# A decoder layer on one core: one list of steps for each engine, and the check of the feed-forward weights on ScalarE

## The reference, cut to what matters

```
z  = layernorm(x)
xs = z shifted by one token
k, v, r = (z*tm + xs*(1-tm)) @ W.T            # three 512x512 products; r through a sigmoid
wkv = recurrence over the tokens (k, v, decay, first), per channel
x1 = x + (r * layernorm(wkv)) @ Wo.T
y  = second recurrence over the tokens with k = layernorm(x1), v = ctx, per channel
xf = x1 + y
out = xf + down( silu(gate(z4)) * up(z4) ),   z4 = layernorm(xf)
```

## Time and profile before

| | |
|---|---|
| median of 3 runs | 647.29 us (646.05 to 648.07) |
| profiled execution | 647.78 us, span 645.7 us |
| TensorE busy | 549.5 us (85% of the span), 2658 products |
| VectorE busy | 524.5 us (81%), 935 instructions |
| ScalarE busy | 312.7 us (48%), 508 instructions, of them 57 table loads, 73.1 us |
| GpSimd busy | 23.9 us (4%) |
| granted TensorE clock, mean | 0.937 of full speed |
| chain that ended last | TensorE 40%, VectorE 35%, issue 15%, ScalarE 7% |

### The profile page before, as it was taken

The page is one execution under the profiler, slowest core; times in us unless marked ns, Lnnn a source line. Parts: engine busy times, 40 slices in busy tenths (PEclk is TensorE's granted clock), DMA queues, the critical chain, the costliest instruction groups (busy, mean ns, idle before and its releaser), DMA issues.

```text
span 645.7 us, 8051 instructions
## 1 busy us (share of the span) xinstructions
PE 549.5 (85%) x2658; PEld 388.7 (60%) x2658; DVE 524.5 (81%) x935; ACT 312.7 (48%) x508; POOL 23.9 (4%) x39
## 2 busy tenths in 40 slices
PE   3997572279999997789999998789999998799995
PEld 2442331166455776777454767677454767689995
DVE  5999998958998579977999579978999679994433
ACT  4426203237555337736564327745664417753231
POOL 1000000001000000001000000001000000000000
PEclk9999696569999998899999998899999998899999
DMA  8999100010020000020001000011001000000000
GB/s 315 383 358 366 60 1 0 0 34 33 0 62 4 2 32 1 1 67 33 0 17 48 1 16 16 1 65 34 1 3 62 1 3 30 0 33 2 17 17 35
DMA packets 11886, 34.72 MB, mean 54 GB/s; under 512 B 912, under 2 KB 912, under 8 KB 11664
## 3 DMA queue, kind: packets, MB, share of 16 engines
q1 hardware_dynamic: 11856, 34.37, 14.9%
HBM read 30.18 MB, written 12.85 MB: 67 GB/s over the span
## 4 chain that ended last, share of the span: by engine, by line
PE 40%; DVE 35%; issue 15%; ACT 7%; DVEq 1%; DMA 1%; POOL 0%; ACTq 0%; SPq 0%; POOLq 0%
PE gu L467 14%; PE dacc L390 9%; PE bank L376 6%; PE bank L443 6%; PE bank L365 4%; DVE t_slot L668 4%; DVE t_otile L848 2%; DVE t_st L789 2%; DVE t_slot L732 2%; DVE t_stats L641 2%; DVE t_pmax L711 2%; DVE t_slot L740 2%; DVE t_slot L796 2%; DVE t_st L735 2%; DVE t_gap L714 1%
## 5 line engine op out<-in xcount | busy, mean ns | idle before, releaser
L467 PE MATMUL gu<-t_z4h,t_gate 128*128 128x256 f32 x352 | 99.4, 312 | 21.5 <-DVE t_h L830 19.4
L467 PE MATMUL gu<-t_z4l,t_gate 128*128 128x256 f32 x352 | 92.4, 293 | 0.0
L467 PE MATMUL gu<-t_z4h,t_up 128*128 128x256 f32 x352 | 90.3, 288 | 0.0
L467 PE MATMUL gu<-t_z4l,t_up 128*128 128x256 f32 x352 | 90.0, 287 | 0.0
L467 PEld LDWEIGHTS gu<-t_z4h,t_gate 128*128 128x128 f32 x352 | 71.0, 202 | 29.7 <-DVE t_h L830 23.1
L597 ACT ACTIVATE t_silu<-gu,t_fsc 128x256 f32<-128x256 f32 x88 | 41.2, 477 | 91.3 <-PE gu L467 91.0
L390 PE MATMUL dacc<-t_down,t_hh 128*128 128x512 f32 x176 | 73.6, 418 | 5.7 <-DVE t_hl L684 5.7
L489 ACT ACT_TABLE_LOAD x57 | 73.1, 1283 | 1.7 <-PEq L912 0.7
L467 PEld LDWEIGHTS gu<-t_z4l,t_gate 128*128 128x128 f32 x352 | 71.0, 202 | 3.4 <-issue 2.2
L390 PE MATMUL dacc<-t_down,t_hl 128*128 128x512 f32 x176 | 71.7, 407 | 0.0
L830 DVE SCALAR_TENSOR_TENSOR t_h<-gu,t_fsc,t_silu 128x256 f32<-128x256 f32 x88 | 41.8, 477 | 36.4 <-ACT t_silu L597 36.0
(11 more groups left out here) (102 smaller groups left out, 897.3 us busy)
## 6 DMA issues: line engine op xcount, KB each, us to landing
t_xres<-in_x SPq DMA_DIRECT2D x8, 512.0 KB, 3.6
t_mixv<-in_ctx_t SPq DMA_DIRECT2D x4, 1024.0 KB, 5.3
out<-t_otile SPq DMA_DIRECT2D x16, 256.0 KB, 2.1
gate_words<-in_gate_t SPq DMA_DIRECT2D x1, 2816.0 KB, 17.7
up_words<-in_up_t SPq DMA_DIRECT2D x1, 2816.0 KB, 24.0
t_gate<-gate_words SPq DMA_DIRECT2D x1, 2816.0 KB, 16.2
down_words<-in_down_t SPq DMA_DIRECT2D x1, 2816.0 KB, 23.3
t_up<-up_words SPq DMA_DIRECT2D x1, 2816.0 KB, 23.8
```

Of the source, the lines that this page charges most:

```text
L467: last = pe.matmul(gu[u % 2][:, side, :], as_read(w[:, k, i * P:(i + 1) * P], exact), as_read(part[:, k, hf * HALF:(hf + 1) * HALF], exact ...
```

## The change

Each engine gets three lists of its own, for the first pass, the loop and the last stretch, and runs through these; the steps that it had no part in are not in them. The check is done on ScalarE: six copies (`weigh0` to `weigh5`), each of one half of a weight tile's low half words (2816 per partition, every second 16-bit word), converted, written as bytes into the output tile, and summed on the way into one column of `low_sums`; VectorE's `weigh` is one maximum over the six columns. `flag` now stands before `y` for TensorE and before `stat4_0` for VectorE. The instructions of all other steps are unchanged. The lists for GpSimd and SP give these two the order that they had; those of the last stretch are left out below, except for one line of TensorE's.

```diff
-F32R_LOST = (1 << 12) - 1
+U16 = mybir.dt.uint16
+U8 = mybir.dt.uint8
...
-    BODY = """
-        prod0 up0 silu0 xf_2 prod1 xf_3 silu1 up1 up2 rest0 up3 rest1 high0 high1 prod2 down0 silu2
-        silu3 stat4_1 turn4_1 high2 up4 stat1_0 z4_1 stat1 down1 prod3 turn1 high3 silu4 silu5 up5
-        rest2 mix_k mix_v rest3 down2 kv0 prod4 kv1 kv2 front0 back0 mix_r up6 high4 part0 high5
-        prod5 down3 up7 front1 back1 silu6 part1 fin0 front2 fin1 kv3 back2 silu7 prod6 part2 front3
-        back3 r0 part3 r1 rest4 r2 up8 r3 fin2 fin3 down4 tanh0 turn2 silu8 down5 down6 tanh1 tanh2
-        tanh3 rest5 prod7 prod8 high6 up9 high7 up10 rest6 stat2 high8 return2 rest7 rest8 rw silu9
-        prod9 down7 down8 wo up11 down9 x1_0 high9 down10 silu10 high10 prod10 up12 silu11 rest9
-        rest10 x1_1 x1_2 x1_3 stat3 turn3 prod11 silu12 out0 high11 xfront0 up13 prod12 silu13 up14
-        up15 rest11 silu14 xback0 prod13 down11 xpart0 high12 prod14 down12 xfront1 xfin0 rest12
-        rest13 high13 xfront2 xback1 down13 up16 up17 up18 down14 silu15 high14 xpart1 prod15 xback2
-        silu16 silu17 up19 rest14 xfin1 prod16 xpart2 xfront3 high15 prod17 xfin2 high16 rest15
-        silu18 silu19 xback3 prod18 xpart3 down15 rest16 up20 down16 high17 high18 high19 silu20
-        silu21 prod19 xfin3 y rest17 high20 rest18 up21 xf_0 xf_1 rest19 prod20 down17 down18
-        stat4_0 down19 prod21 rest20 high21 rest21 turn4_0 down20 z4_0 down21 out1
-        """.split()
-    FIRST_ORDER = """
-        stat1_0 stat1 turn1 mix_k mix_v kv0 kv1 kv2 mix_r front0 back0 part0 kv3 front1 fin0 back1
-        part1 r0 r1 front2 fin1 back2 part2 r2 front3 tanh0 r3 fin2 back3 part3 weigh0 tanh1 tanh2
-        fin3 weigh3 turn2 tanh3 stat2 weigh6 weigh9 weigh12 return2 rw weigh15 weigh18 weigh21
-        weigh24 weigh27 weigh30 wo x1_0 x1_1 x1_2 x1_3 stat3 turn3 xfront0 xfront1 xback0 xpart0
-        xback1 xfin0 xfront2 xpart1 xback2 xfin1 xfront3 xpart2 xback3 xpart3 xfin2 xfin3 y xf_0
-        xf_1 stat4_0 turn4_0 weigh flag z4_0
-        """.split()
...
+    PE_FIRST = """
+        turn1 kv0 kv1 kv2 kv3 r0 r1 r2 r3 turn2 return2 wo turn3 flag y turn4_0
+        """.split()
+    PE_BODY = """
+        up0 up1 up2 turn4_1 up3 up4 turn1 up5 up6 kv0 down0 down1 down2 kv1 kv2 kv3 r0 r1 r2 r3 up7
+        turn2 down3 up8 up9 return2 down4 wo down5 down6 turn3 up10 up11 down7 down8 up12 up13 up14 up15
+        down9 down10 up16 down11 up17 down12 down13 up18 up19 down14 down15 down16 up20 y up21 down17
+        down18 down19 turn4_0 down20 down21
+        """.split()
+    ACT_FIRST = """
+        stat1 turn1 mix_r front0 front1 part0 part1 front2 tanh0 front3 tanh1 tanh2 part2 part3 tanh3
+        weigh0 stat2 rw weigh1 weigh2 weigh3 weigh4 weigh5 stat3 xfront0 xfront1 xpart0 xpart1 xfront2
+        xfront3 xpart2 xpart3 stat4_0 z4_0 flag
+        """.split()
+    ACT_BODY = """
+        silu0 silu1 stat4_1 silu2 z4_1 high0 high1 high2 silu3 stat1 silu4 turn1 silu5 mix_r front0
+        silu6 high3 front1 high4 part0 part1 front2 front3 part2 tanh0 tanh1 tanh2 part3 tanh3 silu7
+        silu8 stat2 silu9 high5 high6 rw high7 high8 high9 stat3 xfront0 xfront1 silu10 silu11 high10
+        xpart0 silu12 silu13 high11 xpart1 silu14 silu15 high12 high13 xfront2 silu16 silu17 high14
+        high15 xfront3 xpart2 high16 silu18 silu19 high17 xpart3 high18 high19 silu20 silu21 high20
+        stat4_0 high21 z4_0
+        """.split()
+    DVE_FIRST = """
+        stat1_0 stat1 mix_k mix_v mix_r front0 front1 back0 part0 back1 fin0 part1 front2 fin1 back2
+        front3 part2 back3 part3 fin2 fin3 stat2 rw x1_0 x1_1 x1_2 x1_3 stat3 xfront0 xfront1 xback0
+        xpart0 xback1 xpart1 xfin0 xfront2 xfin1 xback2 xfront3 weigh xpart2 xback3 xpart3 xfin2 xfin3
+        xf_0 xf_1 flag stat4_0 z4_0
+        """.split()
+    DVE_BODY = """
+        xf_2 xf_3 prod0 stat4_1 stat1_0 prod1 prod2 z4_1 stat1 rest0 prod3 rest1 prod4 rest2 mix_k mix_v
+        front0 mix_r back0 front1 part0 back1 fin0 part1 front2 fin1 back2 front3 part2 prod5 back3
+        rest3 part3 rest4 fin2 fin3 prod6 prod7 stat2 rw x1_0 x1_1 x1_2 rest5 prod8 rest6 rest7 prod9
+        x1_3 stat3 rest8 rest9 xfront0 xfront1 xback0 prod10 prod11 xpart0 rest10 xback1 prod12 prod13
+        xpart1 xfin0 xfront2 xfin1 rest11 rest12 prod14 prod15 out0 xback2 rest13 rest14 xfront3 prod16
+        prod17 xpart2 xback3 rest15 rest16 xpart3 prod18 prod19 xfin2 xfin3 rest17 rest18 xf_0 xf_1
+        rest19 prod20 stat4_0 prod21 rest20 rest21 z4_0 out1
+        """.split()
...
+        low_sums = sb("low_sums", 6)
+        spill = otile[:, :, :].rearrange("p a b -> p (a b)").bitcast(U8)
...
-        def run_first(step):
-
-            for s in FIRST_ORDER:
+        def run_first(step, orders):
+
+            for s in orders[0]:
                 step(s, 0, None)
 
-        def run_rest(eng, step):
+        def run_rest(eng, step, orders):
 
             with eng.Fori(1, B) as b:
-                for s in BODY:
+                for s in orders[1]:
...
+                elif s.startswith("weigh") and s[5:]:
+
+                    n = int(s[5:])
+                    name, tile = (("gate", gate), ("up", up), ("down", down))[n // 2]
+                    if n % 2 == 0:
+                        act.wait_ge(w_in[name], 16)
+                    if n:
+                        act.wait_ge(bits_done, n)
+                    words = tile[:, :, :].rearrange("p a b -> p (a b)")
+                    some = words.shape[1] // 2
+                    low = words[:, n % 2 * some:(n % 2 + 1) * some].bitcast(U16)[:, 0::2]
+                    act.activation(spill[:, 0:some], low, ACT.Copy, accum_out=low_sums[:, n:n + 1]).then_inc(bits_done, 1)
...
-                elif s.startswith("weigh") and s[5:]:
-
-                    for n in range(int(s[5:]), int(s[5:]) + WEIGHED):
-                        name, tile = (("gate", gate), ("up", up), ("down", down))[n // NI]
-                        if n % NI == 0:
-                            dve.wait_ge(w_in[name], 16)
-                        k = n % NI * D
-                        words = tile[:, :, :].bitcast(I32).rearrange("p a b -> p (a b)")[:, k:k + D]
-                        if n < 2:
-                            dve.tensor_scalar(low_bits[:, n % 2, :], words, F32R_LOST, None,
-                                              ALU.bitwise_and).then_inc(bits_done, 1)
-                        else:
-                            dve.wait_ge(bits_done, n - 1)
-                            dve.tensor_tensor(low_bits[:, n % 2, :], low_bits[:, n % 2, :], words,
-                                              ALU.bitwise_or).then_inc(bits_done, 1)
                 elif s == "weigh":
-                    n = 3 * NI
-                    dve.wait_ge(bits_done, n)
-                    dve.tensor_tensor(low_bits[:, 0, :], low_bits[:, 0, :], low_bits[:, 1, :],
-                                      ALU.bitwise_or).then_inc(bits_done, 1)
-                    dve.wait_ge(bits_done, n + 1)
-                    dve.tensor_scalar(low_bits[:, 0, :], low_bits[:, 0, :], F32R_LOST, None,
-                                      ALU.bitwise_and).then_inc(bits_done, 1)
-                    dve.wait_ge(bits_done, n + 2)
-                    dve.reduce_max(inexact[:, :], low_bits[:, 0, :], AXIS_X).then_inc(inexact_done, 1)
+                    dve.wait_ge(bits_done, 6)
+                    dve.reduce_max(inexact[:, :], low_sums[:, :], AXIS_X).then_inc(inexact_done, 1)
                 elif s == "flag":
 
...
+    PE_LAST = """
+        up0 up1 up2 up3 up4 up5 down0 down1 down2 down3 up6 up7 up8 turn4_1 up9 up10 down4 down5 down6
...
```

More of the change, by code:

```diff
@@ L82, in decoder_layer @@
-    LATE = ["xf_2", "xf_3", "stat4_1", "turn4_1", "z4_1"]
-    FFN_STEPS = {f"{s}{u}" for s in ("up", "silu", "prod", "rest", "high", "down") for u in range(NU)}
-    F_STEPS = [s for s in BODY if s in FFN_STEPS or s in LATE or s in ("out0", "out1")]
-    EARLY = [s for s in BODY if s not in F_STEPS]
-    WEIGHED = 3
-    assert FFN_STEPS < set(F_STEPS) and len(BODY) == len(set(BODY)) and set(EARLY) < set(FIRST_ORDER)
+    FFN_KINDS = ("up", "silu", "prod", "rest", "high", "down", "out")
+    LATE = ["xf_2", "xf_3", "stat4_1", "turn4_1", "z4_1"]
@@ new lines, in decoder_layer @@
+    DVE_LAST = """
+        prod0 prod1 prod2 rest0 prod3 rest1 rest2 xf_2 xf_3 rest3 prod4 prod5 prod6 rest4 rest5 stat4_1
+        prod7 prod8 rest6 rest7 prod9 z4_1 prod10 rest8 rest9 prod11 prod12 rest10 prod13 rest11 prod14
+        rest12 rest13 prod15 out0 rest14 rest15 prod16 rest16 prod17 rest17 prod18 prod19 prod20 rest18
+        rest19 rest20 prod21 rest21 out1
+        """.split()
+    POOL_FIRST = """
+        stat1_0 stat1 stat2 stat3 stat4_0
+        """.split()
+    POOL_BODY = """
+        stat4_1 stat1_0 stat1 stat2 stat3 stat4_0
+        """.split()
@@ L90, in decoder_layer @@
+    POOL_LAST = """
+        stat4_1
+        """.split()
+    SP_FIRST = """
+        back3
```

(29 more changed lines are left out.)

15 lines of the change are left out of this document (11 added, 4 removed).

## The result

The kernel after takes 616.1 us (median of 4 runs, 615.34 to 617.67), the kernel before beside it 647.56 (4 runs): ratio 0.952, 95% interval 0.949 to 0.955. The forecast of 625.0 had the sign and seven tenths of the gain (22.3 us of 31.5); the measured time lies at the low edge of the range of 616 to 635, inside it by 0.1 us. The profiled execution is the quickest of the four: 615.34 us, span 613.5.

What follows compares the result with a forecast made beforehand. VectorE was taken to bound the first pass; in the turns VectorE and TensorE wait for each other. From 647.8 us, -6.1 - 8.5 - 6.0 - 5.5 = -26.1, with 3.3 given back -22.8, gives 625.0; range 616 to 635.

Steps and rivals of the forecast that it cites:

- First pass: Pass ahead of the loop: 2.8 us won before turn2, 1.9 before rw, 1.5 before x1_3; -6.1 us taken.
- ScalarE's copy: Weight check in the first pass: each of six summing copies takes 2.7 us, hidden up to 3.3 us a pass.
- Rival (c): First pass: ScalarE's check is slow, 4.9 us a copy, x1's normalisation waits 8 us, 633 us in all; chance 0.07.
- Rival (d): ScalarE, first pass and turns: a table load costs twice its row, 1.28 us more, 635 us in all; chance 0.01.
- First turn: Loop's first turn: -8.5 us, as xf_2 and xf_3 fall into VectorE's wait for the first silu.
- Turns two and three: Loop's later turns: -6.0 us and -5.5 us, the third less because its opening was 0.9 quicker before.
- VectorE's jump back takes 2.87 us: Loop's opening: the jump keeps this cost, and TensorE stands 5.1 us before up2 instead of 1.84.
- My walk: Stepping the new engine lists against each other with trace durations; out1 came at 423.3 instead of 429.3 us.
- rival (b): Loop's opening isn't regained: low clock delays turn1 by 1.5 to 3 us in two turns, 628 to 631; chance 0.10.
- The second recurrence: Loop stretch from xfront0 at 378.8 to out1 at 423.3 us; VectorE has 43.3 us to do, TensorE 40.4.
- Rival (a): Second recurrence keeps its old waits: a turn gains only 3 us, the first 5.5, 630.2 in all; chance 0.22.
- Allowance of 3.3 us: Loop turns: 1.1 us a turn given back from the summed gain for waits the list-by-list estimate misses.

Runs made afterwards that it cites:

- e7: The kernel after with 35 tiny VectorE memsets added behind the loop, in the last stretch; 617.9 us, ratio 0.954 to the kernel before.
- e4: The kernel after with prod0 put ahead of xf_2 and xf_3 in VectorE's loop list, as before; 620.0 us, ratio 0.958 to the kernel before.
- e5: The kernel after with 35 tiny VectorE memsets added behind rw of the first pass, ahead of the loop; 623.7 us, ratio 0.965 to the kernel before.
- e9: The kernel after with prod0 first on VectorE, rest0 before stat1 and down0 before turn1 in the loop; 623.6 us, ratio 0.964.

## Why the prediction was right, and where it was short

- **The sign and the mechanism:** right. Raw sum -26.1, measured -32.2.
- **First pass, -6.1 worked out, -8.7 measured.** x1_3 started 7.9 us earlier, not 6.2. Statistics of turn2 stand at 62.63 (63.0 said), rw at 71.30, behind ScalarE's share of rw. wo took 13.97 us for 15.38: in the execution of before its first 2.9 us, from 77.08 on, ran at a granted clock of 0.51, the lower of the two levels, and the rest at 1.00. That need not be the change's: e7 has the first pass of the kernel after, instruction for instruction, and there the first 2.9 us of wo ran at 0.50, wo takes 15.68 and the pass 129.8 instead of 127.1. Up to 2.7 us of this stage is scatter between executions, as much as the miss.
- **ScalarE's copy, 2.7 said:** 2.54 + 0.19, right; 16-bit words with a stride cost what other copies cost an element. Rival (c) is out.
- **The table load costs its row:** 59.34 to 60.63, 1.29, with 65 loads for 57. Rival (d) is out. The Trainium skill's drain of 1.38 us (ScalarE: Activation LUTs, "What ACT_TABLE_LOAD costs") shows in these rows as little as in the earlier trace rows.
- **First turn, -8.5 said, -8.54 measured;** e4 shows that 3.7 of it are xf_2 and xf_3 in the wait for the first silu.
- **Turns two and three, -6.0 and -5.5 said, -7.6 and -7.0 measured.** The step that failed is "VectorE's jump back takes 2.87 us", carried over from the earlier trace rows as if it belonged to the loop. It depends on what stands ahead of it, and the change had taken 37 instructions from there. With the dear jump, in e5, the step holds in detail (a wait of 5.16, 5.1 said), but the turns are 142.9 and 142.8: -4.4 and -3.5, not -6.0 and -5.5. My walk was too hopeful by 1.6 and 2.0, and lost the 1.6 ahead of the second recurrence, which begins 98.3 us behind the loop's entry (364.39 - 266.05) where 96.8 was said: turn1 comes 18.6 us after the loop's entry (284.61 - 266.05) instead of 17.5 as before, and so out1 143.0 us (409.08 - 266.05) where 141.3 was said. All of up2 runs at the low clock there, 0.41 us a product where the others take 0.28, and the 1.0 us lost at turn1 is not won back: a part of rival (b).
- **The second recurrence:** 44.5 us from xfront0 to out1 said (378.8 to 423.3), 44.66 measured. Rival (a) is out: waits of 0.76 and 1.11 us where 3.35 stood.
- **Allowance of 3.3 us:** given back for waits that a walk misses. It was about right for the turns (3.6 too hopeful), and then the jump gave 3.4 a turn, which no term had. So the forecast missed by 8.9 us mainly for the jump: with it dear, e5 takes 623.7, 1.3 from the 625.0. That nearness is partly luck, since the turns were 3.6 too hopeful and the allowance took back 3.3 for waits in general. And that 616.1 still lies in the range is luck as well: its lower end left 5 us for better luck, and no term for the jump.
- **Last stretch:** 0 said, -0.3 measured.

## What to carry to other kernels

A chain that says "issue" for 2 to 3 us at a loop's jump back, with packets on the engine's instruction queue inside the loop, was here a price that belongs to the loop's place in the program: before costing or tuning the loop's head, count the engine's instructions ahead of it, compare the queue's packets turn by turn, and see whether tiny instructions placed in a wait ahead of the loop take it away. Work that an engine must do before a given point costs the same in any order once nothing else is waiting (e4); moving it pays where it fills a wait that is there anyway (xf_2 and xf_3 in the first turn). An estimate of one stage from one execution is no better than that stage's own scatter, here 2.7 us in the first pass.

## What the runs showed of the hardware that I had not expected

- VectorE's jump back costs 0.23 to 0.26 us if no instructions are fetched and 2.75 to 3.09 if they are; on the turn that is 3.3 to 3.5 us in the new lists and 2.6 to 2.8 in the old. A loop of 356 instructions is fetched again in turns two and three (five packets each) or not at all, and 16 instructions more ahead of it decide (217 and 233); between two kernels 5 do (345 and 350). Of the 31.5 us that the change wins, 6.8 (3.3 and 3.5, after against e5) are the jump.
- 128 memsets of one element per partition take 3.15 us, 0.025 each, and vanish in a wait.
- The same wait of TensorE is followed by the low clock in one turn and not in the next (e9: 0.66 and 1.00 over 8.8 us), and the 32 products of wo take 13.97 us in the kernel after and 15.68 in e7, with the same first pass, where the first 2.9 us ran at 0.50.
